# An earlier attention spread and earlier low parts of x in the opening of a two-layer mixture kernel

## The reference, cut to what matters

```python
h = gelu(embedding @ W0 + b0); h = gelu(h @ W1 + b1)
att = softmax(h @ W2 + b2)                               # (64, 8)
agg_w = einsum('bk,koi->boi', att, weight[..., 0])       # one 32x32 mixer per sample
out = einsum('boi,bih->boh', agg_w, x) + (att @ bias_k)[:, :, None]
# then, with x := out
gate_logits = einsum('bsd,ed->bse', x, gate_w)           # 8 experts, top 2, softmax
result = einsum('bsd,od->bso', x, base_w) + base_b
lora_out = einsum('ebsr,eor,bse->bso', einsum('bsd,erd->ebsr', x, lora_A), lora_B, w_full)
x = x + result + 2.0 * lora_out                          # layer 0
# layer 1: a grouped convolution with 9 taps plus a context term, 4 experts, top 2
```

## Time and profile before

| what | value |
|---|---|
| median of 3 runs | 175.52 us (175.31 to 176.21) |
| the profiled execution's own time | 175.43 us |
| its span | 173.7 us |
| PE busy | 166.7 us (96%) |
| PE weight loads busy | 156.1 us (90%) |
| DVE busy | 126.5 us (73%) |
| ACT busy | 86.7 us (50%) |
| POOL busy | 94.3 us (54%) |
| chain that ended last | PE 88%, DVE 6%, ACT 2%, issue 1% |

### The profile page before, as it was taken

The page is one execution under the profiler, slowest core; times in us unless marked ns, Lnnn a source line. Parts: engine busy times, 40 slices in busy tenths (PEclk is TensorE's granted clock), DMA queues, the critical chain, the costliest instruction groups (busy, mean ns, idle before and its releaser), DMA issues.

```text
span 173.7 us, 3103 instructions
## 1 busy us (share of the span) xinstructions
PE 166.7 (96%) x1097; PEld 156.1 (90%) x1097; DVE 126.5 (73%) x259; ACT 86.7 (50%) x204; POOL 94.3 (54%) x98
## 2 busy tenths in 40 slices
PE   7999699999999999999999999999999999999990
PEld 7897589879899999998898999999899999999980
DVE  6535999999955559989996346998997953377661
ACT  4577663996544567533260467322415463236141
POOL 8307009998299999928029299630007696056000
PEclk9999999999999999999999999999999999999998
DMA  5999200364003400000041000000041000000336
GB/s 165 320 396 396 78 0 0 105 215 125 0 0 116 131 0 0 4 0 0 0 176 71 0 0 0 4 0 0 23 160 64 0 0 0 6 0 0 122 124 242
DMA packets 7215, 13.21 MB, mean 76 GB/s; under 512 B 800, under 2 KB 1696, under 8 KB 7200
## 3 DMA queue, kind: packets, MB, share of 16 engines
q1 hardware_dynamic: 6912, 12.75, 21.2%
q10 hardware_dynamic: 288, 0.26, 0.5%
HBM read 8.82 MB, written 4.19 MB: 75 GB/s over the span
## 4 chain that ended last, share of the span: by engine, by line
PE 88%; DVE 6%; ACT 2%; issue 1%; POOL 0%; DVEq 0%; POOLq 0%
PE ps L1109 21%; PE ps L1111 20%; PE ps L1110 20%; PE ps L1201 8%; PE ps L1102 3%; PE ps L1139 2%; PE ps L1122 2%; PE ps L1298 2%; PE ps L1299 2%; DVE xsl L798 1%; PE ps L1182 1%; PE ps L1310 1%; DVE xs L930 1%; PE ps L1213 1%; DVE xp L802 1%
## 5 line engine op out<-in xcount | busy, mean ns | idle before, releaser
L1109 PE MATMUL ps<-xw_h,xTh 128*128 128x264 f32 (+1 forms) x96 | 30.6, 318 | 0.0
L1110 PE MATMUL ps<-xw_l,xTh 128*128 128x264 f32 (+1 forms) x96 | 29.9, 311 | 0.0
L1111 PE MATMUL ps<-xw_h,xTl 128*128 128x264 f32 (+1 forms) x96 | 29.8, 310 | 0.0
L381 POOL TENSOR_TENSOR xTl<-xT_s,xTh 128x512 fp32r<-128x512 f32 x12 | 16.0, 1360 | 21.7 <-ACT xTh L521 13.3
L386 POOL TENSOR_TENSOR zl<-outb,zh 128x340 fp32r<-128x340 f32 x15 | 15.1, 1005 | 14.4 <-ACT zh L556 7.4
L878 DVE TENSOR_TENSOR outb<-ps,s_sb 128x340 f32<-128x340 f32 x16 | 8.2, 510 | 14.5 <-PE ps L1111 10.8
L1109 PEld LDWEIGHTS ps<-xw_h,xTh 128*128 128x128 f32 x96 | 18.1, 188 | 0.4 <-issue 0.2
L1110 PEld LDWEIGHTS ps<-xw_l,xTh 128*128 128x128 f32 x96 | 18.1, 188 | 0.1
L1111 PEld LDWEIGHTS ps<-xw_h,xTl 128*128 128x128 f32 x96 | 18.1, 188 | 0.0
L1201 PEld LDWEIGHTS ps<-mixT,xp 128*128 128x128 f32 x128 | 16.6, 191 | 1.6 <-DVE x1T L865 0.4
L397 POOL TENSOR_TENSOR x1Tl<-x1T,x1Th 128x512 fp32r<-128x512 f32 x12 | 16.6, 1392 | 2.3 <-DVE late L902 2.3
(11 more groups left out here) (232 smaller groups left out, 512.8 us busy)
## 6 DMA issues: line engine op xcount, KB each, us to landing
xT_s<-in_xT_dram SPq DMA_DIRECT2D x16, 256.0 KB, 3.8
out_dram<-outb SPq DMA_DIRECT2D x12, 256.0 KB, 2.3
x1T<-in_wT_dram SPq DMA_DIRECT2D x4, 256.0 KB, 5.3
outb<-in_wrow_dram SPq DMA_DIRECT2D x4, 256.0 KB, 6.2
x1T<-in_az_dram SPq DMA_DIRECT2D x1, 680.0 KB, 7.6
outb<-in_tapw_dram SPq DMA_DIRECT2D x1, 576.0 KB, 3.7
out_dram<-x1T SPq DMA_DIRECT2D x2, 256.0 KB, 2.2
lgw_s<-in_lgw_dram SPq DMA_DIRECT2D x1, 272.0 KB, 4.4
```

The lines of the kernel that those rows point to most:

```text
L381: nc.gpsimd.tensor_tensor(lo[:, c, :], xT_s[:, g % 2, c, :], hi[:, c, :].bitcast(F32), ALU.subtract).then_inc(x_lo[g % 2], 1)
L1109: nc.tensor.matmul(dst, sh, mh, start=start and c == 0, stop=False)
L1110: nc.tensor.matmul(dst, sh, ml, start=False, stop=False)
L1111: last = nc.tensor.matmul(dst, sl, mh, start=False, stop=stop and c == n - 1)
```

## The change

No instruction is added or removed; the order on three engines changes, and one wait of POOL. On PE the transpose and the spread of the attention come directly behind x_logits, ahead of all of chunk 1 of x_base. Two tiles of chunk 2 stand ahead of mix_logits where one stood, and two behind it where three stood. The last two chunks of x_first for group 1 are issued tile by tile and no longer chunk by chunk. On DVE base_low(2) stands ahead of mix_sum. On POOL x_low(1, 2) has no wait for lw_ok any more, and x_low(1, 3) waits until all four base_low are done.

```diff
@@ POOL @@
             bias_rows(0)
-
-            pool.wait_ge(lw_ok, 1)
             x_low(1, 2)
+
+            pool.wait_ge(base_lo, DC)
             x_low(1, 3)
             bias_rows(1)
@@ DVE @@
             x_low(2)
+            base_low(2)
             dve.wait_ge(attb_mm, 1)
             dve.wait_ge(in_mixw, 16)
             mix_sum(1, prods[0], 0, TG)
-            base_low(2)
@@ PE @@
             x_logits(3)
-            x_base(0, 0, (1,))
-            x_base(0, 1, (1,))
             pe.wait_ge(att_ok, 1)
             nc.tensor.transpose(attT_b, att_n[:, :], ident[0:NB, 0:NB]).then_inc(attT_mm, 1)
...
-            x_base(0, 2, (1,))
-            x_base(0, 3, (1,))
+            for t in range(TG):
+                x_base(0, t, (1,))
             pe.wait_ge(attT_ok, 1)
             pe.wait_ge(in_mixw, 16)
             nc.tensor.matmul(mixb_b, mixw_s[0:K0, M_B:M_B + P], attT[:, :], start=True, stop=True).then_inc(mixb_mm, 1)
             x_base(0, 0, (2,))
+            x_base(0, 1, (2,))
             pe.wait_ge(mixb_ok, 1)
             for t in range(TG):
                 mix_logits(0, t)
-            for t in range(1, TG):
-                x_base(0, t, (2,))
+            x_base(0, 2, (2,))
+            x_base(0, 3, (2,))
...
             turn_lw(0)
-            for c in (2, 3):
-                for t in range(TG):
-                    x_first(1, t, (c,))
+            for t in range(TG):
+                x_first(1, t, (2, 3))
```

## The result

The changed kernel takes 173.69 us, median of 5 runs (173.68 to 174.26), against 175.65 us for the kernel before in 5 runs. The ratio is 0.9896 with a 95% interval of 0.9876 to 0.9915: faster by 1.8 us (1.5 to 2.2). The forecast was 174.0 us, a gain of 1.5.

The account below looks back on a forecast made before the run. PE, busy 96% of the span, was taken as the bound. Its opening stretch gains 1.55 us, taken as 1.5 for p0_out: span 173.7 to 172.2, this execution 175.43 to 173.9, median 174.0 us; range 173.6 to 174.4.

Parts of the forecast that it names:

- PE's stretch: PE from the attention transpose to the first x_first: reordered work sums to 10.42 us, so PE gains 1.55 us.
- The hole: PE's 1.3 us wait for xw_l (base_low(2)) before the first chunk 2 tile, forecast to vanish.
- near tie at p0_out: ACT's first p0_out done at 23.9 us, x_first needs it at 24.0; worth at most 0.2 us.
- The locks: DVE operations reading two SBUF tensors wait for a whole POOL pass; x_low(3) held, costing DVE 0.8 us.
- The forecast for the gates: DVE's gates and lw move 0.6 us earlier, after the lock on x_low(3).
- Rival (a): Mixbias copies on DVE are held by POOL passes, so the gain is only 0.75 us: 174.8 us; chance 0.10.
- Rival (c): POOL's x_low(1,3) falls into DVE's gates, holding the first comparison 1.25 us: about 175.2 us; chance 0.10.
- DVE's sum: DVE gain up to the first bias_x: 0.6 at the gates plus 0.98 from an unheld bias_low(0), 1.58 us.
- keep their distance: Around bias_x and make_y, DVE gains 1.58 us and PE 1.55, so their relative timing is unchanged.
- 0.3 us wait at mix_logits of group 1: PE's wait for the last bias_x, forecast to stay at 0.3 us.
- rival (b): x_low(3) beats POOL's x_low(1,2) or overlaps less; DVE further ahead, gain 1.85 us: 173.7 us; chance 0.12.
- (d): Slower: POOL's phase shifts in the stretch ending at turn_mw, two more DVE subtractions held: 176.6 us; chance 0.08.

Follow-up runs that it names:

- e6: Changed kernel with the last two chunks of x_first for group 1 issued chunk by chunk, as before; 173.90 us, ratio 0.9900 to the kernel before.
- e8: Changed kernel with x_low(3) ahead of the mixbias copies on DVE, and POOL waiting for it before bias_rows(0); 174.35 us, ratio 0.9921 to the kernel before.
- e10: Kernel of e7, but POOL's x_low(1,2) waits until base_low(2) is done; 174.61 us, ratio 0.9943 to the kernel before.
- e11: Changed kernel with bias_x(0,3) ahead of make_x1(0,2) on DVE; 174.10 us, ratio 0.9915 to the kernel before.
- e4: Changed kernel with POOL as before: x_low(1,2) and x_low(1,3) behind lw_ok; 174.24 us, ratio 0.9924 to the kernel before.
- e5: Kernel of e4, also with the last two chunks of x_first chunk by chunk, as before; 174.71 us, ratio 0.9945 to the kernel before.
- e1: Kernel before with the POOL part alone: x_low(1,2) free of lw_ok, x_low(1,3) behind base_lo; 175.98 us against 175.63, ratio 1.0046.
- e3: Kernel before with only base_low(2) moved ahead of mix_sum on DVE; 175.04 us, ratio 0.9980.
- e7: Changed kernel with base_low(2) behind mix_sum again on DVE; 177.22 us, ratio 1.0060 to the kernel before.
- e9: Kernel of e7 with 8 unread matmuls of 240 columns in PE's hole before chunk 2; 175.78 us, ratio 1.0013 to the kernel before.
- e12: Changed kernel with POOL's x_low(1,2) behind base_lo, x_low(1,3) behind bias_low(0), and x_first's last two chunks chunk by chunk; 173.53 us, ratio 0.9882 to the kernel before.
- e2: Kernel before with only the attention transpose and spread moved directly behind x_logits on PE; 174.91 us, ratio 0.9963.

## Why the prediction was right

**PE's stretch.** The forecast was 10.42 us from the transpose to x_first; it took 24.58 − 14.26 = 10.32. From the mark, the transpose begins 1.95 us behind it where the first x_base began 1.76 behind it, so x_first moved by 13.74 − 12.27 = 1.47 and not 1.55. The hole was filled as forecast. The near tie at p0_out cost nothing: PE has no wait for it.

**The locks.** x_low(3) was held: 1.16 us against 0.69. I had about 1.5; it took less because DVE came to it later in POOL's pass. Two errors cancel here, and that is luck: I had DVE ready for x_low(3) 1.4 us earlier than before and set 0.8 us against that for the lock. In fact the mixbias copies ahead of it waited 0.75 us for PE's mixbias matmul (the row at 18.11), so DVE was ready only 7.69 − 6.56 = 1.13 us earlier from the mark, and the lock cost 0.47. The forecast for the gates was −0.6, and they came at −0.67.

The mixbias copies ran in 0.72 us beside that pass, which started 0.08 us behind them, against 0.71 with POOL idle. Rival (a) is refuted. The Trainium skill, "VectorE: DVE Perf Modes", section "Why PSUM operands drop a tier", says that PSUM has only one DVE read port, so that the mode which needs both SBUF read ports is closed to such a copy. The trace agrees, with 0.72 us.

The gates' first comparison began at 22.02, exactly where x_low(1,3) ended (20.71 + 1.31), with its usual 0.42 us. Rival (c) missed by nothing, but it missed. That was less of a coin toss than it looks: the POOL pass is released by base_low(3), and the logits follow base_low(3) on DVE, so the two start together; in e6, e8, e10 and e11 too the comparison began 0.01 to 0.03 us behind the end of that pass. bias_low(0) took 0.68 us as forecast, and DVE's sum was 0.67 + 0.98 = 1.65 against 1.58.

**The step that was mis-sized.** I wrote that the two engines "keep their distance" and that the 0.3 us wait at mix_logits of group 1 "stays". It did not: DVE gained 1.65 and PE 1.47, and the difference came out of that wait. The table shows which of the two counts. x_first stands at −1.47 in the changed kernel, e4, e5 and e6 alike, but mix_logits at −1.66, −1.15, −1.14 and −1.64, each time where bias_x stands. Only where DVE is early enough does PE decide: in e1, e3, e7, e9, e10 and e12 no wait is left before mix_logits, and its shift is 0.35 to 0.39 us better than that of x_first (e11 has another order on DVE there). So in the changed kernel the term that sets the time is DVE's chain to bias_x, 1.65, and not PE's hole, which I used. The forecast was 0.15 us short for it; the rest of the distance to the measured 1.8 lies within the interval.

**The rivals left.** The median of 173.69 us lies on the number of rival (b), 173.7, rather than on my 174.0, and the times can't tell the two apart. The trace stands between them: −1.65 to −1.68 from the mark, x_low(3) held, but less than forecast, and about half of the 0.3 us wait gone. (b) in full, more from DVE, is what e12 makes real; there mix_logits stands at −1.86, as (b) had it, 0.2 us more than in the changed kernel. (d), a worse phase in the later stretch, did not occur: the wait at turn_mw is 0.2 us as before. But its mechanism is real, and it struck in the opening of e7 and e8.

## What to carry to other kernels

Before moving a DVE operation with two SBUF inputs, look up what POOL does at the new place: 0.68 us became 1.45, 1.66 or 2.66 here, and a move on PE alone (e2), which I had put at 1.4 us, gave 0.65 because of it. When PE has a hole, ask what else arrives when it ends; here one cure alone gave 0.65, another 0.35, both 1.3, and the POOL half 0.5 more. When two engines meet at a wait, a gain of one of them counts only until the other comes last. Compare traces from a mark that lies ahead of the edit, not from the span's start.

## What the runs showed of the hardware

A DVE operation with two SBUF inputs was held through two POOL passes that followed each other, bias_rows(0) and x_low(1,2), in e7 (2.66 us), e9 (2.68) and e8 (2.09), and through one when they stood apart (1.44 in e10). In the kernel before, bias_low(0) began 0.56 us into the first of two x_low passes and took 1.66 us, while the pair took 3.36 and not 2.54: there DVE came in between. The product at 65.18 in the same trace is a second such case. It ended at 66.84, 0.55 us behind the first POOL pass, and the pass directly behind that one took 1.36 us where its like took 0.91:

```profile
63.38 0.91 POOL L386 TENSOR_TENSOR zl<-outb,zh 128x340 fp32r<-128x340 f32 x1
...
66.25 1.36 POOL L386 TENSOR_TENSOR zl<-outb,zh 128x340 fp32r<-128x340 f32 x1
```

Why DVE came in between two passes there and not between bias_rows(0) and x_low(1,2) is open; no run tells it.

The kernels in which PE stood still for about 2 us (1.9 in e7's profile, 2.2 in e1's) had in 8 and 4 of 12 executions a mean clock of 0.990 or less, and took 1 to 2 us more in them. The kernel before, with 1.3 us in its profile, had no such execution among the 18 beside e1. The fall to 1.2 GHz itself is seen in one trace, that of e1.
